# Attention over edges: the two additions of a step made one, the step's sum ahead of the dots, and ScalarE's part of the softmax behind its weighing

## The chip, the cores and the metric

The kernel runs on one core of a Trainium2 chip. The metric is the device time of one execution in microseconds (us), the median of several runs. The core's engines run side by side and meet at semaphores: TensorE (PE, with its weight loads PEld), VectorE (DVE), ScalarE (ACT), GpSimd (POOL, which here also issues the indirect gathers) and SyncE (SP, which issues the plain transfers).

## The reference, cut to what matters

A graph of 6250 nodes and 100,000 edges, sorted by target node. A weighted neighbour sum with a layer norm comes first, then two attention layers over the same edges, then a layer norm. The change lies in the attention layers:

```
def _tconv(x, src, dst, edge_attr, Wq, bq, Wk, bk, Wv, bv, We, Ws, bs):
    q = (x @ Wq + bq).reshape(n, H, C)          # H = 4 heads, C = 64
    k = (x @ Wk + bk).reshape(n, H, C)
    v = (x @ Wv + bv).reshape(n, H, C)
    e = (edge_attr @ We).reshape(-1, H, C)
    kj = k[src] + e
    vj = v[src] + e
    logits = jnp.einsum('ehc,ehc->eh', q[dst], kj) / np.sqrt(C)
    m = jax.lax.stop_gradient(jax.ops.segment_max(logits, dst, num_segments=n))
    ex = jnp.exp(logits - m[dst])
    denom = jax.ops.segment_sum(ex, dst, num_segments=n)
    a = ex / (denom[dst] + 1e-16)
    agg = jax.ops.segment_sum(vj * a[:, :, None], dst, num_segments=n)
    return agg.reshape(n, H * C) + x @ Ws + bs
```

All of it is in float32.

## The kernel before

`build` runs a setup and a weighted edge pass, a node pass, the first attention edge pass (names `e_...`), a node pass, the second attention edge pass (the same names) and a last node pass. `edge_pass_attention` goes over T = 832 steps of 128 edges; each step has its edges on the 128 partitions and belongs to one block of 128 target nodes. 26 steps (`BATCH`) make a batch, which shares one softmax; a pass has 32 batches.

Every engine has its own program for the same loop over i, written out by hand, and I call one turn of it a slot. No scheduler reorders anything: an engine issues its instructions in this order and stops at each `wait_ge`.

In slot i:

- POOL gathers the key and value rows of the step's sources, 512 columns, into one of 6 buffers `kv` (L1303). Once in four steps it compares target numbers with partition numbers for four steps at once (`pick`, L1294).
- PE multiplies the edge attributes of the next step by We (L1315, L1316) into one of two banks, `e_e`, except that each fourth step has its edge term loaded ready-made (`made`). Then it picks the next step's queries (L1325), which needs the dots of the step before the present one. Last it makes the sum of an older step (L1366), step i - LAG - 1, the mask times the weighed values; LAG is 42.
- DVE adds the edge term to the keys (L1416) and to the values (L1420), takes four dots with the queries, one for each head (L1428, two instructions each), and adds the sum of step i - LAG - 2 to the accumulator (L1510, in `add_sums`). Then come, in some slots, a skip block's bias (L468, first pass only, 49 blocks) and a part of the softmax.
- ACT makes the mask of step i - LAG (L1561, L1567) and weighs its values with the softmax's exponents, four heads (L1571).

The softmax of a batch is spread over the 16 slots after its last step: even numbered slots hold its steps 0 to 7. Step 0 transposes the logits on PE and copies them on ACT (L1543). Steps 1, 3 and 5 are DVE's scans, which find the maxima over runs of edges with the same target. In step 6 DVE subtracts the maximum (L1474) and ACT takes the exponent (L1546). In step 7 PE transposes back, ACT copies the result (L1551) and makes a factor (L1554). In ACT's program this part of a slot stands ahead of the slot's weighing.

Values stay in NV = 44 buffers of `kvj` until they are weighed, and keys in two more buffers of the same tensor. Weighed values go through R = 4 buffers, so ACT may be four steps ahead of PE's sum.

## Time and profile before

| | us |
|---|---|
| median of 3 runs | 4820.88 |
| lowest and highest | 4820.83, 4821.61 |
| the profiled execution | 4832.06 |
| its span, from the first to the last instruction | 4830.3 |

In the profiled execution PE is busy for 87% of the span, DVE for 83%, ACT for 62% and POOL for 65%. These are averages over passes with different work; ACT's, for one, has little to do outside the attention passes, which begin near 1365 us and 3120 us and end near 2960 us and 4695 us. A start-to-start distance within one engine is shorter than the duration of an instruction where the next one begins before the last has ended, so costs are read from starts.

### The profile page before, as it was taken

To read this page: it belongs to the slowest core of one execution; us is meant where nothing else is said; L and a number is where in the kernel's file an instruction comes from. 1 tells how busy PE (TensorE), PEld (TensorE's weight loads), DVE (VectorE), ACT (ScalarE), POOL (GpSimd) and SP (SyncE) were. 2 spreads that over 40 slices of the span, in tenths; PEclk is the share of its full clock that TensorE was granted. 3 is DMA by queue.
4 is the path that set the end of the run, shared out by engine and by line. 5 is a ranking of instruction groups with operands and counts; after the bars stand their busy time and mean duration, and the time that the engine had idled before them with its cause. 6 is when DMAs were issued, how large, how long until landed. Compare 5 with 4: busy or idle time off the path is not lost. (4 is left out here: it accounts for less than half of the span.)

```text
span 4830.3 us, 107746 instructions
## 1 busy us (share of the span) xinstructions
PE 4189.2 (87%) x17694; PEld 3210.6 (66%) x17694; DVE 3989.0 (83%) x22772; ACT 2982.2 (62%) x10607; POOL 3116.4 (65%) x2996
## 2 busy tenths in 40 slices
PE   2887887888979999999999998889999999999988
PEld 2766666675547777777777774567777777777755
DVE  4655555556869999999999998789999999999986
ACT  1111111112319898989898984149999999989971
POOL 6677777740067777777777771287777777777730
PEclk9999999999999999999999999999999999999989
DMA  4666666654568887878788773587777777777734
GB/s 121 189 192 196 192 193 193 191 167 149 169 212 237 233 236 232 233 229 236 231 234 228 231 230 104 173 247 231 226 230 228 231 228 227 226 228 231 226 114 149
DMA packets 663064, 996.73 MB, mean 206 GB/s; under 512 B 99667, under 2 KB 489690, under 8 KB 662407
## 3 DMA queue, kind: packets, MB, share of 16 engines
q0 software_dynamic: 171408, 540.40, 38.1%
q1 hardware_dynamic: 491000, 449.44, 30.8%
q14 instruction: 471, 3.86, 0.3%
q8 instruction: 185, 3.03, 0.3%
HBM read 870.01 MB, written 119.44 MB: 205 GB/s over the span
## 5 line engine op out<-in xcount | busy, mean ns | idle before, releaser
L1303 POOL DMA_INDIRECT e_kv<-kv,src x1664 | 1635.0, 983 | 748.1 <-DVE e_kvj L1420 449.7
L1571 ACT ACTIVATE e_vals<-e_kvj,e_ex 128x65 f32<-128x65 f32 x6572 | 1725.1, 334 | 5.5 <-PE e_sum L1366 5.1
L1366 PE MATMUL e_sum<-e_vals,e_mask 128*128 128x260 f32 x3328 | 1063.7, 403 | 206.2 <-ACT e_vals L1571 190.0
L1325 PE MATMUL e_q<-q,e_pick 128*128 x3328 | 1017.2, 387 | 95.3 <-DVE e_logit L1428 66.4
L1428 DVE CUSTOM_DVE_ANT_0 e_kvj<-e_kvj,e_q 128x64 f32<-128x64 f32 x6656 | 1060.2, 214 | 3.4 <-PE e_q L1325 2.2
L152 POOL DMA_INDIRECT e_x<-x_rows,e_src x783 | 747.3, 954 | 263.1 <-issue 172.3
L1366 PEld LDWEIGHTS e_sum<-e_vals,e_mask 128*128 128x128 f32 x3328 | 563.0, 190 | 454.4 <-issue 379.7
L1325 PEld LDWEIGHTS e_q<-q,e_pick 128*128 128x128 f32 x3328 | 618.2, 191 | 252.4 <-issue 169.9
L1315 PE MATMUL e_e<-e_we,e_ea 112*128 112x256 f32 x2496 | 752.3, 382 | 17.4 <-DMA e_ea<-attr_tiles 16.2
L1316 PE MATMUL e_e<-e_we,e_ea 112*128 112x256 f32 x2496 | 745.8, 380 | 0.0
L1510 DVE TENSOR_TENSOR acc<-acc,e_sum 128x260 f32 x1664 | 697.3, 419 | 41.4 <-issue 23.6
L530 ACT ACTIVATE q<-e_edges 128x512 f32<-128x512 f32 x208 | 124.2, 597 | 925.5 <-PE e_edges L523 921.7
L1294 POOL TENSOR_SCALAR e_pick<-e_spots,own 128x512 f32<-128x512 bf16 x416 | 660.9, 1589 | 15.4 <-DMA e_spots<-locals 1.1
L1567 ACT ACTIVATE e_mask<-e_apart,one 128x128 f32<-128x128 f32 x1580 | 634.6, 402 | 52.5
L597 PE MATMUL e_sum<-e_x,e_mask 128*128 x1664 | 455.2, 400 | 210.6 <-DVE e_mask L612 114.0
L620 DVE TENSOR_TENSOR acc<-acc,e_sum 128x256 f32 x832 | 349.9, 421 | 332.0 <-PE e_sum L597 308.0
L1561 ACT ACTIVATE e_apart<-iota,local 128x128 f32<-128x128 f32 x1580 | 610.4, 386 | 0.0
L1416 DVE TENSOR_TENSOR e_kvj<-e_kv,e_e 128x256 f32<-128x256 f32 x1248 | 513.4, 411 | 66.2 <-DMA e_kv<-kv,src 40.3
L1315 PEld LDWEIGHTS e_e<-e_we,e_ea 112*128 112x128 f32 x2496 | 477.7, 192 | 96.4 <-issue 20.3
L1420 DVE TENSOR_TENSOR e_kvj<-e_kv,e_e 128x256 f32<-128x256 f32 x1248 | 514.7, 412 | 21.0 <-ACT e_vals L1571 20.6
L1428 DVE DVE_READ_ACCUMULATOR2_ANT e_logit<- 128x1 f32 x6656 | 531.6, 80 | 0.2 <-issue 0.2
L597 PEld LDWEIGHTS e_sum<-e_x,e_mask 128*128 128x128 f32 x1664 | 316.9, 198 | 312.2 <-issue 270.2
(223 smaller groups left out, 4479.1 us busy)
## 6 DMA issues: line engine op xcount, KB each, us to landing
e_ea<-attr_tiles SPq DMA_DIRECT2D x1248, 112.0 KB
edges<-q SPq DMA_DIRECT2D x208, 256.0 KB
e_spots<-locals SPq DMA_DIRECT2D x416, 128.0 KB
e_made<-edges SPq DMA_DIRECT2D x416, 128.0 KB
e_kv<-kv,src POOLq DMA_INDIRECT x1664
kv<-n_proj_rows SPq DMA_DIRECT2D x98, 256.0 KB
q<-attr_tiles SPq DMA_DIRECT2D x208, 112.0 KB
n_x<-x_rows SPq DMA_DIRECT2D x98, 128.0 KB
```

The source lines that it names most:

```text
L152: e.indirect_dma_start(out=self.x[:, at:at + D], out_offset=None, **rows_of(self.t["x_rows"], self.src[:, i:i + 1])).then_inc(self.got[i / ...
L597: e.matmul(sums[i % SUMS][:, 0:D], mask[:, i % R, :], rows, start=True, stop=True).then_inc(summed, 1)
L1294: e.tensor_scalar(pick[:, c % 2, :], spots[:, c % 2, :], k["own"][:, 0:1], None, ALU.is_equal).then_inc(picked, 1)
L1303: e.indirect_dma_start(out=kv[:, u, :], out_offset=None, **rows_of(kv_rows, k["src"][:, i:i + 1])).then_inc(kv_got[u], 16)
L1315: e.matmul(pe_e[a % 2][:, 0:D], ea[:, a % NE, 0:P], we[:, 0, :], start=True, stop=False)
L1316: e.matmul(pe_e[a % 2][:, 0:D], ea[:, a % NE, P:2 * P], we[:, 1, :], start=False, stop=True).then_inc(e_done, 1)
L1325: e.matmul(pe_q[i % 2][:, 0:D], pick[:, c, at:at + P], rows, start=True, stop=True).then_inc(q_done, 1)
L1366: e.matmul(sums[n % 2][:, 0:VALS], mask[:, n % R, :], vals[:, n % R, :], start=True, stop=True).then_inc(summed, 1)
L1428: dot = e.tensor_tensor_reduce(kvj[:, i % 2, h, 0:C], kvj[:, i % 2, h, 0:C], pe_q[i % 2][:, hs], 1.0, 0.0, ALU.mult, ALU.add, logit[:, j % ...
L1510: e.tensor_tensor(rows, rows, sums[n % 2][:, 0:VALS], ALU.add).then_inc(added, 1)
L1567: e.activation(mask[:, n % R, :], apart[:], ACT.Relu, bias=k["one"][:, 0:1], scale=-1.0).then_inc(masked, 1)
L1571: by_weight = e.activation(vals[:, n % R, h * HV:(h + 1) * HV], kvj[:, 2 + n % NV, h, :], ACT.Copy, scale=ex[:, b % 2, h, r:r + 1])
```

## The change

On DVE the two additions of a step become one instruction. Its input is the whole gathered row seen as 2 x 4 x 64, the edge term is read twice through a stride of zero, and the output goes to the key buffer and the value buffer at once (a step of `value_at - key_at` buffers). One semaphore, `kvj_done`, takes the place of `kj_done` and `vj_done` everywhere. The addition now waits for the value buffer (`weighed`) as a whole. `logits` is split into `add_edges` and `dots`, and `add_sums` stands between them. On ACT the softmax part of a slot moves behind the slot's weighing. PE, POOL and SP keep their instructions and their order.

```
-                    e.tensor_tensor(kvj[:, i % 2, :, 0:C], kv[:, i % NG, 0:D].rearrange("p (h c) -> p h c", h=H), edge,
-                                    ALU.add).then_inc(kj_done, 1)
                     if i >= NV:
                         e.wait_ge(weighed, i - NV + 1)
-                    e.tensor_tensor(kvj[:, 2 + i % NV, :, 0:C], kv[:, i % NG, D:].rearrange("p (h c) -> p h c", h=H), edge,
-                                    ALU.add).then_inc(vj_done, 1)
-                    e.wait_ge(kj_done, i + 1)
+                    e.tensor_tensor(kvj[:, key_at:value_at + 1:value_at - key_at, :, 0:C],
+                                    kv[:, i % NG, :].rearrange("p (a h c) -> p a h c", a=2, h=H),
+                                    edge.unsqueeze(1).to_broadcast([P, 2, H, C]), ALU.add).then_inc(kvj_done, 1)
+
+                def dots(i):
+                    j, r = i // BATCH, i % BATCH + 1
+                    e.wait_ge(kvj_done, i + 1)
                     e.wait_ge(q_done, i + 1)
...
                 for i in range(END):
                     if i < T:
-                        logits(i)
+                        add_edges(i)
                     if LATE <= i - LAG < T:
                         late_part(i - LAG)
                     if 0 <= i - LAG - 2 < T:
                         add_sums(i - LAG - 2)
+                    if i < T:
+                        dots(i)
                     if i in due:
                         skip.add(e, due[i])
...
             @block.scalar
             def _(e):
                 for i in range(END):
-                    j, step = step_at(i)
-                    if step == 0:
...
                         by_weight.then_inc(weighed, 1)
+                    j, step = step_at(i)
+                    if step == 0:
```

A plain slot of the first attention pass on DVE, before. L1416 and L1420 are the two additions, the ISA pairs L1428 the dots, L1510 the sum:

```order
L1416 TENSOR_TENSOR e_kvj<-e_kv,e_e 128x4x64
L1420 TENSOR_TENSOR e_kvj<-e_kv,e_e 128x4x64
L1428 ISA e_kvj,e_logit<-e_kvj,e_q 128x64
L1428 ISA e_logit 128x1
L1428 ISA e_kvj,e_logit<-e_kvj,e_q 128x64
L1428 ISA e_logit 128x1
L1428 ISA e_kvj,e_logit<-e_kvj,e_q 128x64
L1428 ISA e_logit 128x1
L1428 ISA e_kvj,e_logit<-e_kvj,e_q 128x64
L1428 ISA e_logit 128x1
L1510 ISA
L1510 TENSOR_TENSOR acc<-acc,e_sum 128x260
```

The same engine and place in the changed kernel, where L1418 is the wide addition, L1512 the sum and L1430 the dots:

```order
L1418 TENSOR_TENSOR e_kvj<-e_kv,e_e 128x2x4x64
L1512 ISA
L1512 TENSOR_TENSOR acc<-acc,e_sum 128x260
L1430 ISA e_kvj,e_logit<-e_kvj,e_q 128x64
L1430 ISA e_logit 128x1
L1430 ISA e_kvj,e_logit<-e_kvj,e_q 128x64
L1430 ISA e_logit 128x1
L1430 ISA e_kvj,e_logit<-e_kvj,e_q 128x64
L1430 ISA e_logit 128x1
L1430 ISA e_kvj,e_logit<-e_kvj,e_q 128x64
L1430 ISA e_logit 128x1
```

The sum moved from behind the dots to ahead of them, and one addition is gone.

ACT around a batch's exponent (softmax step 6) and the two instructions of step 7, first attention pass, before. `e_apart` and `e_mask` make a step's mask, `e_vals` are its four weighings:

```order
L1546 ACTIVATE e_lr<-e_lr 128x128
L1561 ACTIVATE e_apart<-iota,local 128x128
L1567 ACTIVATE e_mask<-e_apart,one 128x128
L1571 ACTIVATE e_vals<-e_kvj,e_ex 128x65 x4
L1561 ACTIVATE e_apart<-iota,local 128x128
L1567 ACTIVATE e_mask<-e_apart,one 128x128
L1571 ACTIVATE e_vals<-e_kvj,e_ex 128x65 x4
L1551 ACTIVATE e_ex<-e_back 128x128
L1554 ACTIVATE e_scale<-e_scale 1x4
```

The same place in the changed kernel, from the weighing of the slot that holds step 6:

```order
L1548 ACTIVATE e_apart<-iota,local 128x128
L1554 ACTIVATE e_mask<-e_apart,one 128x128
L1558 ACTIVATE e_vals<-e_kvj,e_ex 128x65 x4
L1569 ACTIVATE e_lr<-e_lr 128x128
L1548 ACTIVATE e_apart<-iota,local 128x128
L1554 ACTIVATE e_mask<-e_apart,one 128x128
L1558 ACTIVATE e_vals<-e_kvj,e_ex 128x65 x4
L1548 ACTIVATE e_apart<-iota,local 128x128
L1554 ACTIVATE e_mask<-e_apart,one 128x128
L1558 ACTIVATE e_vals<-e_kvj,e_ex 128x65 x4
L1574 ACTIVATE e_ex<-e_back 128x128
L1577 ACTIVATE e_scale<-e_scale 1x4
```

The first three instructions, the weighing of the slot itself, stood behind the exponent before and stand ahead of it now; the others follow in the same order.

## Rows read from the trace of the kernel before

**Rows 1.** The page, part 2: busy tenths in 40 slices of the span, two engines

```profile
DVE  4655555556869999999999998789999999999986
ACT  1111111112319898989898984149999999989971
```

**Rows 2.** Windows: us, busy us by engine (x instructions), clock, DMA share, GB/s

```profile
1483.04:2895.26 1412.22, 1295.62 (x5747) 1030.19 (x5746) 1343.44 (x8833) 1272.59 (x4640) 1039.33 (x943) 1.00 0.80 232
3243.24:4626.62 1383.38, 1262.33 (x5568) 993.86 (x5567) 1332.29 (x8788) 1271.74 (x4641) 1040.94 (x944) 1.00 0.77 228
```

**Rows 3.** Waits, 1443:2860, last row 3203:4590: us in total, times, longest

```profile
POOL e_kv L1303 <- DVE e_kvj L1420: 226.5, 297, 3.1
...
ACT e_lr L1546 <- DVE e_lr L1474: 84.3, 29, 4.3
PE e_sum L1366 <- ACT e_vals L1571: 82.9, 132, 1.7
...
DVE e_block_rows L468 <- PE e_back L460: 26.4, 32, 1.6
...
ACT e_lr L1546 <- DVE e_lr L1474: 67.7, 29, 3.3
```

**Rows 4.** Timeline, ACT, second pass: start, us, instruction, idle before and releaser

```profile
4436.42 0.31 ACT L1546 ACTIVATE e_lr<-e_lr 128x128 f32<-128x128 f32 x1 [2.18 <-DVE e_lr L1474]
4436.64 0.39 ACT L1561 ACTIVATE e_apart<-iota,local 128x128 f32<-128x128 f32 x1
...
4438.32 0.39 ACT L1561 ACTIVATE e_apart<-iota,local 128x128 f32<-128x128 f32 x1
...
4440.68 0.28 ACT L1551 ACTIVATE e_ex<-e_back 128x128 f32<-128x128 f32 x1 [0.58 <-PE e_back L1353]
...
4440.95 0.39 ACT L1561 ACTIVATE e_apart<-iota,local 128x128 f32<-128x128 f32 x1
...
4461.90 0.28 ACT L1543 ACTIVATE e_lr<-e_small 128x128 f32<-128x128 f32 x1 [0.63 <-PE e_small L1333]
4462.07 0.39 ACT L1561 ACTIVATE e_apart<-iota,local 128x128 f32<-128x128 f32 x1
...
4484.48 0.31 ACT L1546 ACTIVATE e_lr<-e_lr 128x128 f32<-128x128 f32 x1 [2.08 <-DVE e_lr L1474]
```

**Rows 5.** Timeline, DVE, right behind the exponent at 4436.42

```profile
4438.45 0.42 DVE L1420 TENSOR_TENSOR e_kvj<-e_kv,e_e 128x256 f32<-128x256 f32 x1 [0.16 <-ACT e_vals L1571]
```

**Rows 6.** Timeline, PE, the same place

```profile
4438.56 0.68 PE L1366 MATMUL e_sum<-e_vals,e_mask 128*128 128x260 f32 x2 [1.39 <-ACT e_vals L1571]
```

**Rows 7.** Timeline, DVE, a slot without waits, second pass

```profile
4450.33 0.41 DVE L1416 TENSOR_TENSOR e_kvj<-e_kv,e_e 128x256 f32<-128x256 f32 x1
4450.66 0.41 DVE L1420 TENSOR_TENSOR e_kvj<-e_kv,e_e 128x256 f32<-128x256 f32 x1
4450.99 0.21 DVE L1428 CUSTOM_DVE_ANT_0 e_kvj<-e_kvj,e_q 128x64 f32<-128x64 f32 x1
...
4451.56 0.42 DVE L1510 TENSOR_TENSOR acc<-acc,e_sum 128x260 f32 x1
4451.89 0.42 DVE L1416 TENSOR_TENSOR e_kvj<-e_kv,e_made 128x256 f32<-128x256 f32 x1
```

**Rows 8.** Timeline, DVE, first node pass

```profile
1200.98 0.67 DVE L744 TENSOR_TENSOR n_proj_rows<-n_proj,n_b_proj 128x512 f32<-128x512 f32 x1
1201.57 0.15 DVE L664 RECIPROCAL n_rs<-n_rs 128x1 f32<-128x1 f32 x1
```

**Rows 9.** Timeline, PE, a slot without waits, first pass

```profile
2059.75 0.60 PE L1315 MATMUL e_e<-e_we,e_ea 112*128 112x256 f32 x2
...
2061.50 0.60 PE L1315 MATMUL e_e<-e_we,e_ea 112*128 112x256 f32 x2
```

**Rows 10.** Timeline, POOL, four gathers between two comparisons

```profile
2034.13 1.58 POOL L1294 TENSOR_SCALAR e_pick<-e_spots,own 128x512 f32<-128x512 bf16 x1
...
2040.71 1.59 POOL L1294 TENSOR_SCALAR e_pick<-e_spots,own 128x512 f32<-128x512 bf16 x1
```

More of the change, by code:

```diff
@@ L1185, in edge_pass_attention @@
         w_got, cleared, ones_set = ph.sem("w_got"), ph.sem("cleared"), ph.sem("ones_set")
[L1186 to L1187 removed]
+        e_done, q_done, kvj_done, dots_done, picked, apart_done = (
+            ph.sem(n) for n in ("e_done", "q_done", "kvj_done", "dots_done", "picked", "apart_done"))
         flat_done, lr_done, fw_done, mx_inner = (ph.sem(n) for n in ("flat_done", "lr_done", "fw_done", "mx_inner"))
```

42 lines of the change are left out of this document (20 added, 22 removed).

## The prediction

> **What bounds the kernel now.** I read the busy slices first [rows 1]. The two attention passes are the stretches where ScalarE (ACT) stands at 8 to 9 tenths; there VectorE (DVE) stands at 9. Outside them nothing is edited. So I cut out the steady part of each pass with the windows view [rows 2]. ACT issues 160 instructions per batch of 26 steps (26 x 6, and 4 of the softmax), and each window holds 4640 or 4641 of them: 29 batches. A batch takes 1412.22/29 = 48.70 us in the first pass and 1383.38/29 = 47.70 in the second. DVE is busy for 1343.44/29 = 46.3 and 1332.29/29 = 45.9 of that, ACT for 43.9, PE for 44.7 and 43.5, POOL for 35.9. No engine is alone in front, so the waits must tell.
>
> The list of waits [rows 3] names ACT's exponent L1546, which waits for DVE's subtraction of the maximum 2.9 us per batch in the first pass (84.3/29) and 2.3 in the second (67.7/29), then, in the first pass, PE's sum L1366, which waits for ACT's weighed values in 132 cases (2.9 us per batch), and DVE's addition of a skip block L468 behind PE (0.9 per batch).
>
> ACT's timeline [rows 4] shows how they hang together. Between the softmax instructions a step follows another in 4438.32 - 4436.64 = 1.68 us with no wait at all: ACT is full. Its floor for a batch is 26 x 1.685 = 43.8, with the exponent 0.22 (4436.42 to 4436.64), the copy L1543 0.17 (4461.90 to 4462.07) and L1551 with L1554 0.27 (4440.68 to 4440.95), up to 0.38 at other places: **44.6 us**. What the batch has above that are ACT's own waits: 47.7 - 44.6 = 3.1 in the second pass, in this batch 2.08 to 2.18 at L1546, 0.58 at L1551 and 0.63 at L1543, each about 0.09 more from start to start. While ACT waits at L1546 it isn't weighing, and the step it owes is the one whose product comes next. Behind it PE's sum waits 1.39 us [rows 6], then DVE's addition to the values 0.16 [rows 5]; a delayed DVE gives the next maximum later, and ACT waits for that. So ACT's floor plus ACT's waits set the pace, and DVE's 45.9 decides how long the waits are.
>
> **Part 1, one wide addition for two.** Removed: per step one of two additions of 128x256. In the undisturbed step of [rows 7] L1416 starts at 4450.33, L1420 at 4450.66, the first dot at 4450.99: 0.66 us for the two, though each lasts 0.41, since the next instruction starts before the last has ended. Added: one addition of 128x512. This program has such an fp32 addition with one operand in PSUM, L744, in the node passes; it starts at 1200.98 and its successor at 1201.57 [rows 8]: 0.59 us. The saving is 0.07 us per step, 1.8 per batch. No row shows this operand form (the edge term read twice by a stride of zero, output in two distant buffers). Its bounds are 0.59 (the nearest row) and 0.82 (two full durations of 0.41, nothing overlapped). I take 0.59, the value of the row of the same operation, type and size, since today's additions already write heads 65 columns apart and still run at a start distance of 0.33. DVE's work becomes 46.3 - 1.8 = 44.5 and 45.9 - 1.8 = 44.1 us per batch, for the first time below ACT's 44.6.
>
 By that rule the merger would save 157 ns per step and the end would lie at ACT's floor, 4605 us (worked out below). The durations nearly agree (0.41 us in [rows 7], 0.67 in [rows 8]), but the starts above are 0.33 apart, so most of that fixed part isn't paid between instructions today, and the sum goes by the starts.
>
> **Part 2, the step's sum between the addition and the dots on DVE.** Nothing is added in work. It hides the end of the wide addition, 0.08 us after the next start, behind the accumulation (0.33 us), so the dots' wait for the addition is free. It costs slack: the sum is wanted 0.57 us (4 dots, 4450.99 to 4451.56) earlier in the slot, and PE's next query, which waits for the dots, gets them 0.33 later. Behind a late sum now stand four dots and, through them, PE's query. The loop closes over two slots: query 0.43, sum 0.43 and 0.25 until its end is seen, accumulation 0.34, dots 0.57, about 2.1 us for two slots of DVE, which itself needs 3.0. It doesn't bind. With a skip block on PE in between (0.87) it is 3.0 against 3.0: there the 0.9 us per batch that L468 waits in the first pass stays, and I leave it in.
>
> The addition now also has ScalarE's weighing of two slots before ahead of its key half. That wait was met 0.33 later; [rows 5] show it at 0.16 where ACT is late.
>
> **Part 3, ACT does its softmax part behind the weighing.** No instruction is added. The wait at L1546 is met one weighing (1.68 us) later, and when it ends, the step that PE needs next is already weighed. By DVE's clock: today ACT begins a slot's weighing 1.57 + 0.2 + 0.3 = 2.1 us after DVE began that slot; afterwards 0.3 after. DVE can go on without a stall as long as ACT's lag stays under about 1.1 to 1.2 (two new slots of 1.50, less 1.68 of weighing; by the sum: two slots and 0.6, less 1.68, less 0.7 on PE). So the stalls right behind L1546 go. From there ACT loses 1.685 - 1.50 = 0.19 per plain slot, some 2 us in the 15 slots until DVE's first scan; that is 1 us more than the cap, and DVE stalls by it. The next 11 slots hold the scans, up to the subtraction. DVE's work beside its steps is 45.9 - 26 x 1.57 = 5.1 us per batch [rows 2, 7], and I put 3.2 of it into these slots, an estimate. They take DVE 11 x 1.50 + 3.2 = 19.7; ACT, from its lag of 1.1, needs 11 weighings, 18.5, so 19.6. What is left of the wait at the exponent is 0.1 to 0.3 us. The waits at L1543 and L1551 (0.6 each, less than 1.68) go wholly. The stalls of DVE then cost nothing: ACT is the late one.
>
> The same reckoning on the kernel before: ACT's lag starts at 2.1, above its cap (about 1.5 with the longer slots), and stays at the cap until the scans. The 11 slots then take DVE 11 x 1.57 and 3.2, 20.5 us. ACT needs 1.5 and ten steps, 18.4, and waits 2.1. With 0.7 at each of the other two places a batch comes to 44.6 + 3.5 = 48.1, against 48.06 from 4436.42 to 4484.48 [rows 4]. That is why I trust it.
>
> **What is next late.** PE: four products of 0.435 us, 2059.75 to 2061.50 [rows 9], 1.74 per plain step, but a quarter of the steps has two, so 6.1 per four steps, against ACT's 6.74. POOL: 6.6 us per four steps back to back (2034.13 to 2040.71 [rows 10]), 42.8 per batch, under 44.6. The DMA engines go from a share of 0.80 and 0.77 to some 0.85 [rows 2].
>
> **The sum.** Second pass: 44.6 and 0.3 left = 44.9, gain 2.8 per batch. First pass: 44.6 and 0.9 left = 45.5, gain 3.2. Thirty batches per pass (the 29, half a batch at the start, 14 steps at the end): 84 + 96 = 180 us. At a pass's start (the first 42 steps) POOL sets the pace and in its last 42 steps the edited additions and dots don't occur: zero, at most 2 us either way. The profiled execution took 4832.06 (span 4830.3), the median is 4820.88; its 11 us more, 0.2%, lie on every part of it alike, so I take the saving off the median: 4821 - 180 = **4641 us**. With nothing left above ACT's floor: (4.1 + 3.1) x 30 = 216, 4605. With 1.5 and 0.9 left: 144, 4677.
>
> **Rivals.**
> - *DVE stays the bound.* The stalls stay as they are, because the sum ahead of the dots takes back what ACT's earlier weighing gives, and only the 1.8 us of work go. For it: 46.3 and 45.9 are the highest busy times, and the summed slack of Part 2 is thin where a skip block stands. Against: ACT has no wait between softmax parts. 1.8 x 60 = 108: 4713, from 4677 to 4735. Perfetto Trace Analysis of the Trainium skill (Identifying the Most-Contended Engine) ranks engines by occupancy and would name DVE (95 and 96%), and give this time; ACT's gapless rows speak against it.
> - *The wide addition saves nothing* (0.66 us). DVE needs 45.9 to 46.3 and 0.5 of stalls: a gain of 1.3 on average, 78 us: 4743.
> - *Slower: the wide addition is dear.* By its stride of zero or its far output it takes 0.80, near the 0.82 bound. DVE then needs 45.9 + 26 x 0.14 = 49.5. It decides from about 0.73, where DVE's work alone reaches 47.7. At 0.80 it is +1.8 per batch, with nothing of ACT's waits in the way: 4821 + 108 = 4929. Against: the two rows at 256 and 512 columns lie on one line.
> - *No change: the gathers bind.* If 232 GB/s were what the queue can bring, a batch would stay. Against: it is the gathers that wait for DVE, 226.5 us in 297 cases [rows 3]. 4821.
>
> **Chances.** Forecast (4605 to 4677) 0.62; DVE the bound 0.18; saves nothing 0.09; dear addition 0.06; gathers 0.05. The range 4605 to 4735 holds the first two, 0.80. A measurement of this kernel can tell 0.2%, some 10 us, from no change. Faster 0.89, within 0.2% 0.05, slower 0.06.
>
> **What would show it.** L1416 and L1420 become one group of 1664 at about 670 to 680 ns, its next instruction 0.59 behind. The exponent's wait falls from 2.9 and 2.3 us per batch to under 1, those of L1543 and L1551 to nothing. A batch takes 45.5 and 44.9 us. ACT stands at 97% or more in the steady windows, DVE keeps about its share with new waits for the sum or for e_vals. Wrong would be: a duration of the addition over 750 ns; DVE idle over 1.5 us per batch while ACT still waits over 1.5 at the exponent (the sum's new place costs); or POOL gathers without a wait and DVE waiting for e_kv.

## The result, and the profile after

| | before | after |
|---|---|---|
| median, us | 4820.85 | 4674.94 |
| runs | 4820.75 to 4821.61 | 4668.24, 4669.62, 4680.27 |
| profiled execution, us (its span) | 4832.06 (4830.3) | 4668.24 (4666.5) |
| a batch of 26 steps, first pass, us | 48.70 | 46.22 |
| a batch of 26 steps, second pass, us | 47.70 | 45.15 |

A fourth run of the new kernel took 9873.25 us, twice the others, and is left out. The ratio is 0.9691, with an interval of 0.9674 to 0.9709: 3.1% faster, 146 us by the medians. The forecast was 4641 us and 180 us. The two passes give (48.70 - 46.22) x 30 + (47.70 - 45.15) x 30 = 74 + 76 = 150 us, so the gain lies in the loops that were edited.

The page after, the 40 slices of VectorE (DVE) and ScalarE (ACT), which answer to [rows 1]:

```profile
DVE  4655555556869999999999998879999999999987
ACT  1111111112316999999999996129999999999970
```

ACT now stands at 9 where it stood at 8 and 9 in turn. The windows over 29 batches of each pass, cut from one start of the exponent to another, answer to [rows 2] and have the same columns (stretch, us, busy us by engine, clock, DMA share, GB/s):

```profile
1482.16:2822.62 1340.46, 1284.60 (x5748) 1029.72 (x5747) 1289.48 (x8079) 1267.25 (x4641) 1040.34 (x944) 1.00 0.83 245
3163.13:4472.60 1309.47, 1250.70 (x5568) 992.26 (x5567) 1276.83 (x8034) 1266.66 (x4640) 1040.53 (x944) 1.00 0.81 241
```

Per batch, DVE is busy 1289.48/29 = 44.46 and 1276.83/29 = 44.03 us. The prediction had 44.5 and 44.1. ACT is busy 43.7 of 46.22 and of 45.15, 94.5% and 96.7% (before 90% and 92%). PE is busy 44.3 of 46.22 in the first pass.

The list of waits answers to [rows 3]. It gives the waiting engine and line, what it waits for, us in total, times and the longest. The lines have moved: the exponent is now L1569, DVE's subtraction L1476, the wide addition L1418, the sum's accumulation L1512, the dots L1430 and ACT's weighing L1558. First pass, 1480 to 2800:

```profile
POOL e_kv L1303 <- DVE e_kvj L1418: 163.6, 287, 2.4
...
ACT e_lr L1569 <- DVE e_lr L1476: 46.8, 29, 2.9
PE e_q L1325 <- DVE e_logit L1430: 46.3, 84, 1.2
DVE e_block_rows L468 <- PE e_back L460: 22.1, 35, 1.0
```

Second pass, 3160 to 4475, same columns:

```profile
PE e_q L1325 <- DVE e_logit L1430: 38.3, 68, 1.0
ACT e_lr L1569 <- DVE e_lr L1476: 19.7, 30, 1.3
...
PE e_sum L1366 <- ACT e_vals L1558: 9.7, 28, 0.5
```

The wait at the exponent fell from 2.9 to 46.8/29 = 1.6 us per batch in the first pass and from 2.3 to 19.7/30 = 0.66 in the second. The sum on PE hardly waits for weighed values any more in the first pass (1.7 us in 5 cases, 82.9 in 132 before). What grew is the wait of PE's query for DVE's dots, to 1.6 us per batch. In the kernel before it was 0.9, in the first pass's window of 29 batches:

```profile
PE e_q L1325 <- DVE e_logit L1428: 26.1, 45, 1.1
```

ACT's timeline in the second pass answers to [rows 4] (start, us, instruction, idle before it and releaser):

```profile
4382.19 0.31 ACT L1569 ACTIVATE e_lr<-e_lr 128x128 f32<-128x128 f32 x1 [0.63 <-DVE e_lr L1476]
4382.41 0.39 ACT L1548 ACTIVATE e_apart<-iota,local 128x128 f32<-128x128 f32 x1
...
4385.78 0.26 ACT L1574 ACTIVATE e_ex<-e_back 128x128 f32<-128x128 f32 x1
...
4406.24 0.25 ACT L1566 ACTIVATE e_lr<-e_small 128x128 f32<-128x128 f32 x1
...
4427.60 0.31 ACT L1569 ACTIVATE e_lr<-e_lr 128x128 f32<-128x128 f32 x1 [0.89 <-DVE e_lr L1476]
```

The copies L1574 and L1566, which had 0.58 and 0.63 us of idle time before them, have none. A batch of ACT now holds one wait, at the exponent. ACT's floor of 44.6 us and that wait give 46.2 and 45.3, and the batches take 46.22 and 45.15. The frame of the prediction, "ACT's floor plus ACT's waits set the pace", closes to some 0.1 us; the size of what is left is where it missed.

DVE's timeline in a slot without waits, second pass, answers to [rows 7] (same columns):

```profile
4385.53 0.67 DVE L1418 TENSOR_TENSOR e_kvj<-e_kv,e_e 128x512 f32<-128x512 f32 x1
4386.13 0.41 DVE L1512 TENSOR_TENSOR acc<-acc,e_sum 128x260 f32 x1
4386.46 0.20 DVE L1430 CUSTOM_DVE_ANT_0 e_kvj<-e_kvj,e_q 128x64 f32<-128x64 f32 x1
...
4387.03 0.67 DVE L1418 TENSOR_TENSOR e_kvj<-e_kv,e_e 128x512 f32<-128x512 f32 x1
```

The wide addition lasts 0.67, and the next instruction starts 0.60 behind it. The slot is 1.50 us, from 1.57.

### Where the missing 30 us are

The prediction's batches were 45.5 and 44.9. The misses are 0.72 x 30 = 22 us in the first pass and 0.25 x 30 = 7 in the second. DVE's own idle time tells where they lie. Here are its groups of instructions over the 29 batches: busy us, mean ns, then idle us just before them and what ended it. Second pass, 3163.13 to 4472.60:

```profile
L1418 DVE TENSOR_TENSOR e_kvj<-e_kv,e_e 128x512 f32<-128x512 f32 x566 | 383.1, 677 | 0.6 <-issue 0.2
L1512 DVE TENSOR_TENSOR acc<-acc,e_sum 128x260 f32 x754 | 314.1, 417 | 16.5 <-PE e_sum L1366 4.6 <-issue 0.7
...
L1506 DVE TENSOR_SCALAR e_rescale<-e_sum 128x4 f32<-128x4 f32 x29 | 4.7, 161 | 4.8 <-PE e_sum L1366 4.5
```

First pass, 1482.16 to 2822.62:

```profile
L1512 DVE TENSOR_TENSOR acc<-acc,e_sum 128x260 f32 x754 | 314.3, 417 | 11.1 <-issue 1.6 <-PE e_sum L1366 1.0
...
L468 DVE TENSOR_TENSOR e_block_rows<-e_back,e_block_bias 128x256 f32<-128x256 f32 x45 | 19.1, 424 | 23.7 <-PE e_back L460 23.1
...
L1506 DVE TENSOR_SCALAR e_rescale<-e_sum 128x4 f32<-128x4 f32 x29 | 4.7, 160 | 5.0 <-PE e_sum L1366 4.8
```

DVE is idle 1340.46 - 1289.48 = 51.0 us in the first pass, 1.76 per batch, and 1309.47 - 1276.83 = 32.6 in the second, 1.13 per batch. 21.3 of the 32.6 lie before the two lines that read a sum, L1512 and L1506. The rest is small gaps between dependent instructions, and how large those are without any waiting is seen in a variant of the new kernel with two narrow additions (below): there DVE was idle 1322.53 - 1311.47 = 11.1 us over 29 batches, 0.38 each. So DVE needs 44.03 + 0.38 = 44.41 us per batch for itself in the second pass and 44.46 + 0.38 = 44.84 in the first. The sum of a batch, on DVE's side:

| us per batch | first pass | second pass |
|---|---|---|
| DVE busy | 44.46 | 44.03 |
| its small gaps | 0.38 | 0.38 |
| wait for the skip block, L468 | 0.82 | 0 |
| wait for a sum, L1512 | 0.38 | 0.57 |
| wait for a sum, L1506 | 0.17 | 0.17 |
| sum | 46.21 | 45.15 |
| measured | 46.22 | 45.15 |

Busy and idle time make up the whole of a window, so this table must close; it tells where DVE stands, and not why. The wait for a sum isn't new either. The kernel before had it too, in its second pass:

```profile
L1510 DVE TENSOR_TENSOR acc<-acc,e_sum 128x260 f32 x754 | 315.8, 419 | 15.9 <-issue 13.1 <-PE e_sum L1366 0.4
```

Counted by slot, about half of those 15.9 us lie in the slots right behind the exponent. In the changed kernel none do, and nearly all of the 16.5 lie in the slots around the start of the next softmax and its scans. In part that is ACT's doing: the 9.7 us that PE's sum still waits for weighed values in the second pass fall in the same slots, where the prediction saw ACT fall behind.

The prediction took DVE's busy time alone, found it under ACT's 44.6 and counted DVE as out of the way. It put the wait for a sum at nothing. And it added the skip block's 0.9 to ACT's 44.6, though it is DVE that stands still in it: 44.84 was the number to add it to.

### The profile page after: what moved, and what is told of

It reads as the page before. It is cut to its first block and busy times, and to the rows that moved or that the text cites. A ratio compares the mean times of both kernels' runs of the same rounds, so it can differ in the third digit from the quotient of the medians.

```text
span 4666.5 us, 107658 instructions
## 1 busy us (share of the span) xinstructions
PE 4159.3 (89%) x17694; PEld 3201.7 (69%) x17694; DVE 3873.8 (83%) x21108; ACT 2969.4 (64%) x10607; POOL 3113.8 (67%) x2996
## 3 DMA queue, kind: packets, MB, share of 16 engines
q0 software_dynamic: 171408, 540.40, 39.3%
## 5 line engine op out<-in xcount | busy, mean ns | idle before, releaser
L1558 ACT ACTIVATE e_vals<-e_kvj,e_ex 128x65 f32<-128x65 f32 x6572 | 1723.2, 334 | 1.3 <-PE e_sum L1366 1.3
L1325 PE MATMUL e_q<-q,e_pick 128*128 x3328 | 1035.1, 392 | 146.4 <-DVE e_logit L1430 111.4
L1430 DVE CUSTOM_DVE_ANT_0 e_kvj<-e_kvj,e_q 128x64 f32<-128x64 f32 x6656 | 1062.5, 214 | 7.6 <-PE e_q L1325 2.7
L1366 PE MATMUL e_sum<-e_vals,e_mask 128*128 128x260 f32 x3328 | 1033.6, 393 | 28.7 <-ACT e_vals L1558 15.3
L1418 DVE TENSOR_TENSOR e_kvj<-e_kv,e_e 128x512 f32<-128x512 f32 x1248 | 845.5, 678 | 44.3 <-DMA e_kv<-kv,src 39.2
L1325 PEld LDWEIGHTS e_q<-q,e_pick 128*128 128x128 f32 x3328 | 594.1, 191 | 376.4 <-issue 302.0
L1512 DVE TENSOR_TENSOR acc<-acc,e_sum 128x260 f32 x1664 | 693.8, 417 | 32.2 <-PE e_sum L1366 9.3
L1366 PEld LDWEIGHTS e_sum<-e_vals,e_mask 128*128 128x128 f32 x3328 | 577.5, 189 | 186.6 <-issue 106.8
L1315 PEld LDWEIGHTS e_e<-e_we,e_ea 112*128 112x128 f32 x2496 | 477.1, 192 | 90.6 <-issue 18.9
L1430 DVE DVE_READ_ACCUMULATOR2_ANT e_logit<- 128x1 f32 x6656 | 532.1, 80 | 0.1
L1316 PEld LDWEIGHTS e_e<-e_we,e_ea 112*128 112x128 f32 x2496 | 471.7, 189 | 68.9
```

What stands on the lines that cost most here:

```text
L1315: e.matmul(pe_e[a % 2][:, 0:D], ea[:, a % NE, 0:P], we[:, 0, :], start=True, stop=False)
L1316: e.matmul(pe_e[a % 2][:, 0:D], ea[:, a % NE, P:2 * P], we[:, 1, :], start=False, stop=True).then_inc(e_done, 1)
L1325: e.matmul(pe_q[i % 2][:, 0:D], pick[:, c, at:at + P], rows, start=True, stop=True).then_inc(q_done, 1)
L1366: e.matmul(sums[n % 2][:, 0:VALS], mask[:, n % R, :], vals[:, n % R, :], start=True, stop=True).then_inc(summed, 1)
L1418: e.tensor_tensor(kvj[:, key_at:value_at + 1:value_at - key_at, :, 0:C], kv[:, i % NG, :].rearrange("p (a h c) -> p a h c", a=2, h=H), edg ...
L1430: dot = e.tensor_tensor_reduce(kvj[:, i % 2, h, 0:C], kvj[:, i % 2, h, 0:C], pe_q[i % 2][:, hs], 1.0, 0.0, ALU.mult, ALU.add, logit[:, j % ...
```

## The experiments

They form three groups, each run on a chip of its own with the kernel before beside it. The kernel before took 4825.89 us in the third group, much like in the comparison above, but 5129.94 in the first and 5153.92 in the second. So each kernel is compared by its difference from the kernel before of its own group, and across groups only with care. The kernel before has a trace on the faster kind of chip only.

| group (before, us) | kernel | us | ratio (interval) | against before | batch, passes 1 and 2 |
|---|---|---|---|---|---|
| 1 (5129.94) | ACT's part alone | 5028.79 | 0.9807 (0.9784 to 0.9831) | -101 | 48.57, 47.72 |
| 1 | wide addition alone | 5185.34 | 1.0103 (1.0078 to 1.0128) | +55 | 51.19, 50.16 |
| 1 | wide addition, sum ahead of dots | 5179.3 | 1.0103 (1.0079 to 1.0127) | +49 | 50.97, 50.05 |
| 1 | after, dots directly behind the addition | 5080.31 | 0.9907 (0.9886 to 0.9929) | -50 | 49.48, 48.80 |
| 2 (5153.92) | after | 5075.95 | 0.9844 (0.9828 to 0.9861) | -78 | 49.35, 48.51 |
| 2 | after, skip blocks in two slots | 5080.04 | 0.9857 (0.9841 to 0.9874) | -74 | 49.29, 48.33 |
| 2 | after, one edge product | 5046.61 | 0.9791 (0.9775 to 0.9808) | -107 | 48.69, 47.74 |
| 2 | after, PE's sum ahead of its query | 5002.2 | 0.9705 (0.9687 to 0.9723) | -152 | 47.92, 47.20 |
| 3 (4825.89) | after | 4668.91 | 0.9672 (0.9656 to 0.9689) | -157 | 46.24, 45.17 |
| 3 | after, two narrow additions | 4698.65 | 0.9737 (0.972 to 0.9753) | -127 | 46.85, 45.60 |
| 3 | after, PE's sum ahead of its query | 4659.31 | 0.9651 (0.9635 to 0.9668) | -167 | 45.87, 45.28 |
| 3 | the same with seven gather buffers | 4684.23 | 0.9701 (0.9683 to 0.9718) | -142 | 46.31, 45.56 |

### ACT's part alone

The kernel before with only the program of ACT changed:

```diff
                 for i in range(END):
-                    j, step = step_at(i)
-                    if step == 0:
...
                     n = i - LAG
                     if 0 <= n < T:
...
                         by_weight.then_inc(weighed, 1)
+                    j, step = step_at(i)
+                    if step == 0:
...
```

> The kernel before with only ScalarE's softmax part moved behind the weighing of its slot; the two narrow additions and the dots ahead of the sum stay. Theory A (ScalarE's floor of 44.6 us per batch plus its own waits set the pace, and VectorE's work decides the waits): the waits at the copy and at step 7 go, the exponent's wait shrinks, VectorE's 45.9 to 46.3 us of work per batch become the bound with about 0.3 to 0.8 of stalls: 46.2 us per batch in the second pass, 47.1 in the first, 4821 - 93 = about 4728 us. Theory B (VectorE's work alone is the bound, stalls stay): no instruction of VectorE goes, 4821 us.

It gave -101 us, near the 93 of theory A; that the softmax part's place has no effect (theory B) is out. The gain repeats beside the wide addition on the same chip: 5185.34 - 5080.31 = 105 us between the second and the fourth row of the table. Theory A's waits are seen only in part. The one at the copy of step 7 is gone, those at the exponent (L1565) and at the copy of step 0 (L1562) are not, in the second pass:

```profile
L1565 ACT ACTIVATE e_lr<-e_lr 128x128 f32<-128x128 f32 x30 | 9.3, 310 | 81.6 <-issue 50.2 <-DVE e_lr L1474 31.5
L1562 ACT ACTIVATE e_lr<-e_small 128x128 f32<-128x128 f32 x29 | 7.9, 271 | 11.1 <-PE e_small L1333 7.5 <-issue 3.3
```

How large they were before the edit on this chip isn't known. DVE has the same instructions as before. The windows (columns as above):

```profile
1692.92:3101.31 1408.39, 1300.63 (x5747) 1023.30 (x5746) 1333.54 (x8833) 1270.04 (x4640) 1036.82 (x943) 1.00 0.79 233
3445.32:4829.07 1383.75, 1268.65 (x5568) 988.46 (x5567) 1318.49 (x8788) 1269.19 (x4641) 1037.73 (x944) 1.00 0.77 228
```

DVE's busy time is still the highest, 46.0 and 45.5 per batch, about what it was before, and yet the kernel is 1.9% faster, though nothing was taken from the work of the most occupied engine.

### The wide addition alone

The kernel before with one addition instead of two, the dots right behind it and the sum where it was:

```diff
-                    e.tensor_tensor(kvj[:, i % 2, :, 0:C], kv[:, i % NG, 0:D].rearrange("p (h c) -> p h c", h=H), edge,
-                                    ALU.add).then_inc(kj_done, 1)
...
+                    e.tensor_tensor(kvj[:, key_at:value_at + 1:value_at - key_at, :, 0:C],
+                                    kv[:, i % NG, :].rearrange("p (a h c) -> p a h c", a=2, h=H),
+                                    edge.unsqueeze(1).to_broadcast([P, 2, H, C]), ALU.add).then_inc(kvj_done, 1)
...
                     if i < T:
-                        logits(i)
+                        add_edges(i)
+                        dots(i)
```

> The kernel before with only the wide addition: dots directly behind it, the sum behind the dots, ScalarE as before. Theory A: the dots now wait for the end of an addition that has just started (0.68 us long, against 0.66 for the two narrow ones from the first start to the dots), with some 0.03 to 0.05 us until the end is seen: 0.71 against 0.66 per step, 1.3 us more per batch on VectorE, and ScalarE's waits unchanged: 4821 to 4890 us, about 4860. Theory B: 1.8 us of work less per batch, 4713 us.

It gave +55 us, in theory A's range. The timeline of DVE shows why (columns as above):

```profile
2201.01 0.68 DVE L1418 TENSOR_TENSOR e_kvj<-e_kv,e_e 128x512 f32<-128x512 f32 x1
2201.72 0.22 DVE L1430 CUSTOM_DVE_ANT_0 e_kvj<-e_kvj,e_q 128x64 f32<-128x64 f32 x1
```

A dot that needs the addition's result starts 0.71 us behind its start. With two narrow additions the first dot stood 0.66 behind the first addition [rows 7], because the value half covered the end of the key half. The merger by itself thus costs 0.05 per step, 0.05 x 26 x 60 = 78 us if every step pays it.

### The wide addition with the sum ahead of the dots, ACT as before

The changed kernel with ACT's block put back ahead of the weighing (the reverse of the first diff).

> The kernel after with ScalarE's program of before (softmax part ahead of the weighing). Theory A: ScalarE still starts the slot behind the exponent late, and the sum is now wanted earlier, so the lag is over its cap and VectorE stalls at once; the exponent's wait stays near 1.8 to 2.5 us and the two other waits of 0.7 stay: a gain of 0.3 us per batch or so, 4800 us (4770 to 4821). Theory B: VectorE's 1.8 us less per batch count, 4713 us.

It gave +49 us where A expected a small gain and B 108 us: both missed. DVE's groups in its second pass (29 batches, columns as above):

```profile
L1418 DVE TENSOR_TENSOR e_kvj<-e_kv,e_e 128x512 f32<-128x512 f32 x566 | 384.4, 679 | 61.0 <-issue 37.0 <-ACT e_vals L1575 19.2 <-DMA e_over<-singles 2.7
L1512 DVE TENSOR_TENSOR acc<-acc,e_sum 128x260 f32 x754 | 315.3, 418 | 67.4 <-PE e_sum L1366 32.6 <-remote 21.7 <-issue 6.0
```

DVE is idle 128 us before these two lines. One reading is that an ACT that stops at the exponent before it has weighed makes the sum late, and that the late sum now holds the four dots and PE's next query with them. The changed kernel on the other slower chip speaks against that as the main cause. There ACT's part has moved, and yet, in its second pass:

```profile
L1512 DVE TENSOR_TENSOR acc<-acc,e_sum 128x260 f32 x754 | 314.5, 417 | 67.7 <-remote 31.3 <-PE e_sum L1366 24.5 <-issue 6.1
```

The same 67 us stand before the accumulation with ACT's part in either place; in the run of this section only some 14 of them lie in the slots right behind the exponent. ("remote" and "issue" are waits whose releaser the profile doesn't show.) The wide addition alone, with the sum behind the dots, has 15.9 there. So on the slower chips it is the sum's new place that costs: against the wide addition alone DVE's busy time falls by 1.9 us per batch in the second pass, its waits grow by 1.8, and the batch by the table changes by 0.1. What ACT's lateness adds is seen before the addition (19.2 us for `e_vals`). On the faster kind this combination wasn't run.

### The changed kernel with the dots directly behind the addition

```diff
                         add_edges(i)
+                        dots(i)
                     if LATE <= i - LAG < T:
...
                         add_sums(i - LAG - 2)
-                    if i < T:
-                        dots(i)
```

> The kernel after with the dots directly behind the wide addition and the sum behind them. Theory A: VectorE pays the end of the wide addition in each step, 0.71 until the first dot in place of 0.59: 3.1 us per batch more than after, 47.2 and 47.6 of work, so VectorE is the bound: 4785 us (4750 to 4810). Rival: the place of the sum only matters for slack (PE gets the dots earlier), and the time is that of the kernel after or better, 4660 to 4675 us.

It gave -50, which fits the range that A gave (4750 to 4810, 71 to 11 under the kernel before). Against ACT's part alone on the same chip it is 5080.31 - 5028.79 = 52 us slower, and the wide addition alone was 55 slower than the kernel before: the same price with and without ACT's move. DVE's group of dots in the second pass shows the price as waits and busy time (29.5 and 480.3 in the run with ACT's part alone on the same chip, whose dots also stand right behind the additions):

```profile
L1430 DVE CUSTOM_DVE_ANT_0 e_kvj<-e_kvj,e_q 128x64 f32<-128x64 f32 x3016 | 486.8, 218 | 51.2 <-DVE e_kvj L1418 26.0
```

### The changed kernel with two narrow additions

```diff
-                    e.tensor_tensor(kvj[:, key_at:value_at + 1:value_at - key_at, :, 0:C],
-                                    kv[:, i % NG, :].rearrange("p (a h c) -> p a h c", a=2, h=H),
-                                    edge.unsqueeze(1).to_broadcast([P, 2, H, C]), ALU.add).then_inc(kvj_done, 1)
+                    e.tensor_tensor(kvj[:, key_at, :, 0:C], kv[:, i % NG, 0:D].rearrange("p (h c) -> p h c", h=H), edge, ALU.add)
+                    e.tensor_tensor(kvj[:, value_at, :, 0:C], kv[:, i % NG, D:].rearrange("p (h c) -> p h c", h=H), edge,
+                                    ALU.add).then_inc(kvj_done, 1)
```

> The changed kernel with the wide addition taken apart again into the two narrow ones, both ahead of the sum, ScalarE's part behind the weighing. Theory A: VectorE has 1.8 us more per batch, 45.9 to 46.3 in place of 44.1 to 44.5; ScalarE's floor of 44.6 no longer sets the pace, VectorE does with some 0.5 of stalls: 46.6 to 47.2 us per batch, 60 to 100 us more than the changed kernel. Rival (where gathers or TensorE are late the wide addition is worth nothing, as the run with ScalarE's edit alone suggests, which lost 1.9% against 1.6% of the whole change on such chips): within 20 us of the changed kernel.

It took 4698.65 beside 4668.91 for the changed kernel on the same chip: the wide addition is worth 30 us, ACT's part and the sum's place together 127. The 30 are less than the 60 to 100 expected. Its window over 29 batches of the second pass:

```profile
3179.82:4502.35 1322.53, 1253.33 (x5566) 989.05 (x5565) 1311.47 (x8788) 1266.64 (x4640) 1040.06 (x944) 1.00 0.80 239
```

And DVE's groups in its second pass, 3179.8 to 4502.35:

```profile
L1512 DVE TENSOR_TENSOR acc<-acc,e_sum 128x260 f32 x754 | 312.8, 415 | 1.5 <-issue 0.4
L1418 DVE TENSOR_TENSOR e_kvj<-e_kv,e_e 128x256 f32<-128x256 f32 x566 | 232.1, 410 | 0.2
```

With two narrow additions DVE hardly waits at all in the second pass. Its busy time is 1311.47/29 = 45.2 of a batch of 45.60 in the second pass: here DVE is the bound. With the wide one its work falls by 1.1 to 1.3 us per batch, but the batch falls by 45.60 - 45.17 = 0.43 and 46.85 - 46.24 = 0.61 only. ACT's floor of 44.6 lies close below, and DVE begins to wait for the sum (1.5 us at L1512 become 16.5). A saving on the bound engine is worth its full size only down to the next engine.

### Placing the skip blocks

In the first pass DVE waits for PE at L468. The variant puts the 49 skip blocks of the changed kernel only in slots 17 and 22 of a batch, where no softmax product stands:

```diff
+            spread = [b * batches // s.blocks for b in range(s.blocks)]
+            skip.due = {BATCH * j + (17 if j not in spread[:b] else 22): b for b, j in enumerate(spread)}
```

> The changed kernel with the 49 skip blocks of the first pass put into slots 17 and 22 of a batch (behind the exponent, ahead of the first scan), where VectorE has time to spare, in place of an even spread. Theory C (what the first pass has above the second comes from skip blocks that fall ahead of the subtraction of the maximum and delay it): the first pass's batch goes from 46.2 to about 45.5 us, 20 us less than the changed kernel. Rival: the skip blocks cost their work on TensorE and VectorE wherever they stand: within 5 us of the changed kernel.

It took 5080.04 beside 5075.95, no gain. DVE's idle time before L468 was 37.5 us over 29 batches of the first pass, against 27.0 for the changed kernel on the same chip. So on this chip the block's place doesn't take its wait away. On the faster kind, where the first pass has 0.72 us per batch to explain, it wasn't run.

### The changed kernel on the second chip, and PE's share

> The changed kernel itself, on the chip on which the next three run. 146 to 152 us less than the kernel before on the same chip, 46.2 us per batch in the first attention pass and 45.2 in the second.

The same kernel gained 78 us, not the 146 to 152 expected, where the fast chips gave 146 and 157. That is less than ACT's part alone gave on the other slower chip (1.6% against 1.9%). The waits at ACT's copy of step 0 are back too, 1.2 and 1.0 us per batch (L1566). Its waits in the first pass, 1702 to 3133, name causes that hardly occur on the fast chip:

```profile
PE e_q L1325 <- DVE e_logit L1430: 87.5, 142, 1.5
ACT e_lr L1569 <- DVE e_lr L1476: 52.4, 17, 4.9
ACT e_lr L1569 <- issue: 43.1, 12, 5.3
DVE e_kvj L1418 <- issue: 29.3, 32, 1.8
```

PE was the suspect. One variant drops the second of the two products of the edge rows:

```diff
-                    e.matmul(pe_e[a % 2][:, 0:D], ea[:, a % NE, 0:P], we[:, 0, :], start=True, stop=False)
-                    e.matmul(pe_e[a % 2][:, 0:D], ea[:, a % NE, P:2 * P], we[:, 1, :],
-                             start=False, stop=True).then_inc(e_done, 1)
+                    e.matmul(pe_e[a % 2][:, 0:D], ea[:, a % NE, 0:P], we[:, 0, :], start=True, stop=True).then_inc(e_done, 1)
```

> The changed kernel with the second of the two products of an edge term left out (so the edge term is half of it; TensorE has 0.43 us less in three of four steps, 8.5 us per batch). Theory D (in the changed kernel TensorE, busy for 44.3 of 46.2 us per batch in the first pass and 43.1 of 45.2 in the second, is what VectorE waits for): both passes go to ScalarE's floor, 44.6 to 44.9 us per batch, 40 to 55 us less than the changed kernel. Rival (the remaining wait at the exponent comes from ScalarE and VectorE alone): within 10 us of the changed kernel.

It was 29 us faster than the changed kernel of its group, between the two expectations. With that work away, PE waits for the dots instead (1700 to 3100, 87.5 us in 142 cases above):

```profile
PE e_q L1323 <- DVE e_logit L1428: 161.2, 185, 2.0
```

So PE's amount of work isn't the bound by itself: 8.5 us less of it per batch, counted by starts (5.2 and 5.4 us of busy time), took 0.7 and 0.8 off the batch. Its order was the next suspect. The query stands at the head of a slot and waits for the dots, which now come one accumulation (0.33 us) later. The sum, which DVE now wants earlier, stands behind it:

```diff
                             edge_product(c * (QUAD - 1) + at)
-                        query(i + 1)
...
+                    if 0 <= i - LAG - 1 < T:
+                        sum_up(i - LAG - 1)
                     j, step = step_at(i)
                     if j is not None:
                         softmax(j, step, i)
-                    if 0 <= i - LAG - 1 < T:
-                        sum_up(i - LAG - 1)
+                    if i + 1 < T:
+                        query(i + 1)
```

> The changed kernel with TensorE's order in a slot changed to fit VectorE's: edge product, skip block, the sum of the older step, softmax transposes, then the next step's query (before: edge product, query, skip block, transposes, sum). Theory D: TensorE's sum no longer stands behind the query that waits for the dots, TensorE can work during VectorE's scans, and VectorE waits less: 45.4 us per batch in the first pass and 44.9 in the second, about 30 us less than the changed kernel. Rival: the order of sum and query doesn't matter, or the query comes too late now: the same or up to 50 us more.

It gained 74 us on the changed kernel, more than the 30 expected, and is at 0.9705 of the kernel before on this chip. The 67.7 us before the accumulation in the second pass became 19.4:

```profile
L1513 DVE TENSOR_TENSOR acc<-acc,e_sum 128x260 f32 x754 | 312.9, 415 | 19.4 <-PE e_sum L1366 9.1 <-issue 5.3 <-remote 3.6
```

On the slower chip the order of PE is worth about as much as the whole change was.

### The same on the faster kind of chip

> The changed kernel again, on the chip of the next three. 0.969 of the kernel before if this chip is like that of the first result, 0.984 if it is like that of the first run of this kernel beside the experiments.

The changed kernel repeats: 4668.91 us, 46.24 and 45.17 per batch.

> The changed kernel with TensorE's sum ahead of the next step's query, as in e8_sum_before_query. 20 to 75 us less than the changed kernel on the same chip: 30 if the chip is like the first one, 74 as measured on the other.

4659.31, 10 us less than the changed kernel and under the 20 to 75 expected. The two intervals overlap on this chip, so here the gain can't be told from none with certainty; with the 74 us on the slower one, this is the version to prefer. The first pass gains 0.37 per batch, the second loses 0.11. DVE's groups in the first pass, with the wide addition as L1419 and the accumulation as L1513:

```profile
L1419 DVE TENSOR_TENSOR e_kvj<-e_kv,e_e 128x512 f32<-128x512 f32 x566 | 383.9, 678 | 9.2 <-issue 5.2 <-PE e_e L1316 0.3 <-DMA e_kv<-kv,src 0.3
L1513 DVE TENSOR_TENSOR acc<-acc,e_sum 128x260 f32 x754 | 312.9, 415 | 1.4
...
L468 DVE TENSOR_TENSOR e_block_rows<-e_back,e_block_bias 128x256 f32<-128x256 f32 x45 | 19.0, 422 | 13.1 <-PE e_back L460 12.7
```

The wait for the sum is gone (11.1 to 1.4), the skip block's is halved (23.7 to 13.1), and 8.6 us come back before the wide addition. The net is -9.7 - 10.6 + 8.6 = -11.7 us over 29 batches, 0.40 each, against the 0.37 measured. So in the first pass the waits for the sum and for the skip block hang on PE's order. In the second pass the wait for the sum turned up mostly before the addition instead:

```profile
L1419 DVE TENSOR_TENSOR e_kvj<-e_kv,e_e 128x512 f32<-128x512 f32 x566 | 383.9, 678 | 12.7 <-issue 7.3 <-PE e_e L1316 0.7
L1513 DVE TENSOR_TENSOR acc<-acc,e_sum 128x260 f32 x754 | 312.7, 415 | 2.3 <-issue 1.3
```

16.5 us before the accumulation became 2.3, and 0.6 before the addition became 12.7. With DVE at 44.5 (44.09 busy and 0.38 of small gaps), ACT at 44.6 and PE at 43.6 us of a batch of 45.28, a wait taken away at one place comes back at another.

A last variant gives the gathers a seventh buffer, at the price of one in the ring R, to see whether the waits before the addition are late gathers:

```diff
-    NV, NG, NE, R = LAG + 2, 6, 5, 4
+    NV, NG, NE, R = LAG + 2, 7, 5, 3
```

> e8_sum_before_query with seven gather buffers in place of six, and, to have the room, three weighed-value buffers in place of four. Theory G (on the slower chips VectorE's addition waits for gathers that land late, seen as waits without a releaser): 1.1 us per batch of such waits goes, 30 to 60 us less than e8 there and nothing on a fast chip. Rival: the waits are not the gathers', or the missing value buffer makes ScalarE wait for TensorE: the same or up to 60 us more than e8.

It was 25 us slower than the same order with six. The buffer given up isn't the reason: ACT waits no more than before anywhere but at the exponent (0.84 us per batch before the mask in both). Nor does DVE wait more, 1.4 and 1.0 us per batch in the two passes against 1.4 and 1.2. Its instructions last longer, 44.93 and 44.52 us per batch against 44.46 and 44.09. Most of it is one group, the wide additions of the steps whose edge term is loaded ready-made. In the second pass, first with six gather buffers, then with seven:

```profile
L1419 DVE TENSOR_TENSOR e_kvj<-e_kv,e_made 128x512 f32<-128x512 f32 x189 | 128.9, 682 | 1.0 <-DMA e_kv<-kv,src 0.5 <-issue 0.3
L1419 DVE TENSOR_TENSOR e_kvj<-e_kv,e_made 128x512 f32<-128x512 f32 x189 | 141.9, 751 | 0.5 <-issue 0.3
```

With seven buffers a good half of these additions overlap POOL's comparison `pick`, 223 of the 416 in the kernel, and those last 792 ns on average, the others 686. With six only 13 touch one, and none lasts over 750 ns. One case with seven:

```profile
2047.54 1.58 POOL L1294 TENSOR_SCALAR e_pick<-e_spots,own 128x512 f32<-128x512 bf16 x1
2047.62 1.17 DVE L1419 TENSOR_TENSOR e_kvj<-e_kv,e_made 128x512 f32<-128x512 f32 x1
```

By the program POOL issues a gather when a buffer comes free, and the comparison stands between two gathers. So one more buffer lets the comparison come one of DVE's steps earlier, next to the step with the ready-made term. The additions whose edge term lies in PSUM (`e_e`) last 677 ns in either case. So this run doesn't tell what a seventh buffer is worth by itself, and whether gathers are short of buffers on the slower kind of chip is open, since it wasn't run there.

## Why the prediction was right, and where its size was off

- **What bounds the kernel.** Right. ACT's waits between its softmax parts were what a batch had above 44.6 us; ACT's move alone gave -101 us on its chip. The Trainium skill (Perfetto Trace Analysis, Identifying the Most-Contended Engine) ranks engines by occupancy, which names DVE; 108 us was the prediction's own estimate for DVE's saved work. In the run with ACT's part alone DVE's work stayed and 101 us went, so as a guide to what a change is worth the ranking doesn't agree with that run. It agrees one step later: once ACT's waits were short, the run with two narrow additions had DVE busy 45.2 of 45.60.
- **Part 1.** The start distance was right (0.60, predicted 0.59), the duration too (678 ns on average, predicted 670 to 680), and DVE's busy time to 0.1 us. The price in time was not: 30 us in the final kernel, where 1.8 x 60 = 108 would have been DVE's work. The prediction never priced the part by itself, since it let ACT's floor cut the sum, and the run with two narrow additions bears that out. The Trainium skill (VectorE: DVE Perf Modes, the section on the TRN2 errata) has (N + 151) cycles at 0.96 GHz for an fp32 tensor_tensor; read as the cost of each instruction, it gives an estimate of 157 ns saved per step. The slot fell by 0.07 us, so the trace doesn't agree with that reading; as a duration the formula's 691 ns is near the 678 measured.
- **Part 2.** Right that the sum hides the addition's end: 0.60 to the sum, 0.71 to a dot in the two variants with the dots behind. Wrong that it costs nothing. PE's query waits for the dots 46.3 us in 84 cases of the first pass (26.1 in 45 before), and the sum stands behind the query on PE. DVE waits 0.55 and 0.74 us per batch for it, where "it doesn't bind" had put nothing. Taking PE's sum out from behind its query gave back 74 us on a slower chip, and on the faster kind 10, all of it in the first pass. On the slower chips the new place costs all that the addition saves, as the third experiment showed. The loop of two slots was closed with plain slots and one skip block, and not with PE's softmax products, DVE's scans or ACT's lag in it; which of these breaks it wasn't taken apart. The prediction's own sign of being wrong here, DVE idle over 1.5 us per batch while ACT still waits over 1.5 at the exponent, came true in the first pass: 1.76 and 1.61.
- **Part 3.** Right in kind on the faster chips: the waits at the two copies went, but for 1.8 us in 3 cases at one of them in the first pass. The wait left at the exponent was mis-sized, 1.6 us in the first pass and 0.66 in the second instead of 0.1 to 0.3. The reckoning on the kernel before that it was trusted for gave 48.1 for one batch of 48.06, but the mean batch is 47.70, and the waits of 0.7 at each copy stand in about every second batch only (15 and 14 of 29), so part of that agreement was luck. Its loss of 0.19 in 15 slots is 2.8 us, not 2; the cap on the lag makes that no difference.
- **What is next late.** Most of the miss lies here. PE was judged by plain steps (6.1 us per four against 6.74), though [rows 2] had it busy 44.7 per batch in the first pass, over ACT's floor. DVE was judged by its busy time without the 0.38 us of gaps that even a DVE without waits has. With them it stands at 44.84 in the first pass, above ACT, and the skip block's wait of 0.82 and the sum's of 0.55 come on top of that.
- **The sum.** 180 us predicted, 146 measured, or 150 by batches. 22 of the 30 missing lie in the first pass, 7 in the second. ACT is busy for 94.5% and 96.7% of the steady windows, under the 97% foretold.
- **The rivals.** *DVE stays the bound* (4713): out as told, though with two narrow additions it is true of what comes next. *The wide addition saves nothing*, *is dear*: out by the start distance of 0.60. The first of these was also summed wrongly: 46.3 and 45.9 with 0.5 of stalls are a gain of 1.9 and 1.3 per batch, 96 us and 4725, not 78 and 4743. *The gathers bind*: out, the rate rose from 232 to 245 GB/s in the first pass, and they still wait for DVE 163.6 us. That is shown for the faster kind of chip; on the slower one the unexplained waits leave it open.

## What to carry to other kernels

Cost an instruction by the distance to the next start, with one number for an independent successor (0.60 here) and one for a dependent one (0.71); a merger that takes away the cover of its own latency can lose, as this one did alone on a slower chip (+55 us). A step that waits for another engine belongs behind the work that others wait for, and when one engine's order is changed, change the order of the engine that feeds it too, as the variant with PE's sum ahead of its query did. When a run with other buffer counts is slower, compare the durations of its instructions before blaming a wait, as the one with seven gather buffers shows. When three engines stand within 3% of each other, compare each one's busy time plus the small gaps that it has even when nothing is late, and add a wait to the engine that stands still in it.

## What the runs showed of the hardware

The same programs ran at two speeds on different chips: the kernel before at 4821 to 4826 us in two comparisons and at 5130 and 5154 on two other chips. The instructions compared were equally long on both in the second pass: the wide addition 678 and 677 ns, the accumulation 417 and 417, ACT's weighing 334 and 334. The wide addition on the second chip, from the page's groups, beside the fast chip's:

```profile
L1418 DVE TENSOR_TENSOR e_kvj<-e_kv,e_e 128x512 f32<-128x512 f32 x1248 | 846.4, 678 | 119.7 <-issue 80.3
```

```profile
L1418 DVE TENSOR_TENSOR e_kvj<-e_kv,e_e 128x512 f32<-128x512 f32 x1248 | 845.5, 678 | 44.3 <-DMA e_kv<-kv,src 39.2
```

What differs is the rate of transfers, above all ahead of the attention. The slices of GB/s of the changed kernel, first on the second chip, then on the fast one:

```profile
GB/s 88 140 164 159 162 164 165 159 161 161 137 168 198 233 230 234 232 230 222 232 229 229 229 227 185 146 201 231 223 224 227 225 224 228 223 224 222 226 141 153
```

```profile
GB/s 117 189 195 193 193 195 193 193 187 132 167 174 258 241 245 248 244 244 243 245 248 243 248 241 127 181 227 243 243 239 241 239 243 243 240 241 242 241 124 155
```

In the projections and node work at the start it is some 162 against 193. In the attention both are over 220, but there the slower chip shows waits whose releaser the profile doesn't name, and its batches are 3.1 and 3.3 us longer. Transfers that land later on these chips would explain both; that was not shown, since the traces don't tell when the gathers land. The time that the packets themselves took speaks neither way: the page's software queue, the gathers' by its 540 MB, gives them 36.6% of 5074.8 us and 39.3% of 4666.5, which is 1857 and 1834 us for each of the 16 DMA engines. The granted clock of TensorE doesn't explain it: it was 1.00 in the steady windows of both.

The wide addition with the ready-made edge term, whose operands all lie in SBUF, lasted longer where POOL compared at the same time: 792 ns on average instead of 686 in the run with seven gather buffers.

The kind of chip matters for the change, which is worth 3.1 to 3.3% on one kind and 1.6% on the other, while the version with PE's order matched is worth 3.5 and 3.0%.
